# A Mamba-2 scan stage: decays spread over the partitions by broadcast loads, and one convolution by taps on ScalarE and VectorE

## The chip, the cores and the metric

The kernel runs on one core of one Trainium2 chip. The metric is the device time of one execution, in microseconds (us); the median of three executions is compared. The core has TensorE (PE; its weight loads are shown as PEld), VectorE (DVE), ScalarE (ACT), GpSimd (POOL) and SyncE (SP, which only issues DMAs here), each with its own in-order instruction queue. They wait for each other through counters.

## What is computed

The input has 32 sequences of 256 tokens of 64 channels. Three layers follow:

- a convolution with 9 taps to 128 features, scaled by a window norm, tanh, bias, relu (248 tokens are left per sequence);
- a Mamba-2 block with a residual, with 4 heads of 64, a state of 64, and a causal convolution of 4 taps ahead of a SiLU;
- a mixture of 16 experts (top 2) with a shared expert and a last feed-forward layer.

The change is in the Mamba-2 block, whose heart is, cut to what matters:

```python
zxbcdt = x @ in_proj_w                       # z 256, xBC 384, dt 4
xBC = silu(causal_conv_4_taps(xBC) + conv_b) # per channel
dt = softplus(dt + dt_bias); decay = exp(-dt * exp(A_log))
def step(h, inp):                            # over the tokens, per head
    h = decay_t * h + (dt_t * x_t) outer B_t
    y_t = h @ C_t
y = (ys + D_skip * x) * silu(z); y = rms_norm(y) * norm_w
out = y @ out_proj_w
```

## The kernel before

The tokens are cut into 16 units of 2 sequences. A sequence has 248 tokens, that is 2 chunks of CH = 124. A unit goes through four stages, each one step behind the other: `a` (the 9-tap convolution, tanh, norm), `b` (the projections, the 4-tap convolution, dt), `c` (the scan and the output projection) and `d` (second norm, router logits, shared expert, scatter of rows to the experts). Step t works on unit t in stage a, t-1 in b, t-2 in c, t-3 in d. The loops `for t in range(STEPS)`, one per engine (PE line 911, ACT 1149, POOL 1368, DVE 1748), write out by hand the order of each engine's work in a step. After the steps come the expert phase (139 blocks of 128 rows) and the last layer.

The scan has no recurrence in the chip's sense. For each sequence (a "part" n of the unit, n = 0, 1) the kernel forms the scores G = B C^T (`scores`, line 760), multiplies them by the product of decays between the two tokens, and takes the product with the inputs (`mix`, 790). The decay products are made as follows. `decays` (774) does 8 TensorE transposes per part: each spreads one head's decays of one chunk (a column of `dec`) over all partitions, in PSUM. `long_scans` (1500) runs two scans of 2x248 elements over them (`state = state * decay + diagonal`), which gives L0 (tokens of chunk 0 against all 248), and `short_scans` (1509) four of 124 elements for L1 (chunk 1 against itself). A `keep` mask of POOL (line 1323) stops the state at the start of each sequence. `decayed_scores` (1516) multiplies L0 (992 elements) and L1 (496 elements) by G, to M0 and M1.

The order of VectorE's step is: long scans of part 0, `dt_first` (1453), `x_rest` (1430), short scans and decayed scores of part 0, `bc_taps` (1480), `dt_rest` (1465), `skip_add` of part 0 (1526), scans and decayed scores of part 1, `stats` of unit a (1442), logits and slots or the first half of `choose` (these two in alternate steps), `skip_add` of part 1, `x_scale`, `shared_out`, `sum_squares`, the second half of `choose` (every other step), `hn_rest` (1435), `mean_squares`, `residual` (which waits for a power on POOL, line 1338), `new_stats`. From `stats` POOL makes the reciprocal deviation (`rstd_of`, 1308), ACT the norm (`norm`, 1051), PE transposes it (`hn_transposes`, 697), ACT copies it (`hnT_copy`, 1069) and DVE takes the low part (`hn_rest`); the next step's projections need it. From `skip_add` of part 1 POOL does `gate` (1326, line 1332), then PE `output` (808, line 814) and after it, in PE's order, `hn_transposes`. POOL's order has `rstd_of` ahead of `gate` of part 1.

The 4-tap convolution: for B and C it is done by taps (`bc_begin` on ACT, `bc_taps` on DVE, `bc_silu` on ACT). For x, two parts of 128 channels each, the taps are folded into the projection weights (`w_tap`), and `projection` (725) does 4 taps x 3 products (high and low parts) = 12 matmuls of 496 columns for each x part (k = 0, 1), and 3 for each z part (k = 2, 3). Lines 650 to 652 are the three matmuls of `product`.

## Time and profile before

| what | value |
|---|---|
| median of 3 executions | 1030.62 us (1022.71, 1030.62, 1031.51) |
| profiled execution, its own time | 1024.98 us |
| its span in the profile | 1023.1 us |
| PE, DVE, POOL, ACT busy | 905.9, 724.6, 587.5, 502.3 us |

Roughly, the steps run to 585 us, the experts to 885 us, and the last layer to the end. "Busy" is the time in which an engine's instructions ran. In the timeline a line's second number is the time in which a run of equal instructions was under way; the next instruction of an engine can begin up to some 0.08 us ahead of the end shown for the last. "Issue" is time for which the profile shows no wait.

### The profile page before, as it was taken

How to read it: one execution, taken by the hardware profiler on the slowest of the kernel's cores; microseconds unless marked ns; L12 is line 12 of the kernel's file. 1: busy time of each engine (PE TensorE's matmuls, PEld its weight loads, DVE VectorE, ACT ScalarE, POOL GpSimd, SP SyncE). 2: the span in 40 equal slices, each digit the busy share in tenths (PEclk: the TensorE clock that was granted, in tenths of full speed). 3: DMA queues.
4: the chain of work that ended last, by engine and by line, in shares of the span. 5: the costliest groups of instructions: out<-in, count | busy, mean ns of one | idle time of the engine just before them, and what ended most of it. 6: DMA issues, size and time to landing. Idle time of an engine off the chain costs nothing.

```text
span 1023.1 us, 22359 instructions
## 1 busy us (share of the span) xinstructions
PE 905.9 (89%) x6324; PEld 790.4 (77%) x6325; DVE 724.6 (71%) x2092; ACT 502.3 (49%) x1259; POOL 587.5 (57%) x649
## 2 busy tenths in 40 slices
PE   4697999999999999999874369999999998669998
PEld 3576877877877787887654269999999998558887
DVE  5357799888889989888874335555555554599993
ACT  3333555554555555555322125555555554555653
POOL 5435455777778777777646454444444444365551
PEclk9989999999999999999966679999999999879999
DMA  7400000110100110000095112232221221224332
GB/s 180 90 11 11 1 11 12 31 31 22 30 17 27 32 31 27 16 19 16 18 275 158 40 44 68 78 85 67 65 67 55 58 64 54 56 81 114 97 101 51
DMA packets 72057, 59.12 MB, mean 58 GB/s; under 512 B 19169, under 2 KB 61468, under 8 KB 71985
## 3 DMA queue, kind: packets, MB, share of 16 engines
q1 hardware_dynamic: 63440, 41.88, 15.9%
q0 software_dynamic: 8544, 16.34, 4.8%
q8 instruction: 37, 0.61, 0.3%
q14 instruction: 36, 0.29, 0.1%
HBM read 35.62 MB, written 23.81 MB: 58 GB/s over the span
## 4 chain that ended last, share of the span: by engine, by line
PE 48%; DVE 24%; issue 15%; POOL 8%; another core or an unknown queue 1%; ACT 1%; DMA 1%; SPq 0%; DVEq 0%; POOLq 0%; ACTq 0%
PE psum L967 13%; PE psum L952 13%; DVE arena L1504 4%; DVE arena L1852 4%; PE psum L650 3%; POOL x_slots L1362 3%; PE psum L651 3%; PE psum L652 3%; PE psum L785 2%; PE psum L802 2%; DVE h_all L1552 2%; DVE arena L1857 2%; PE psum L961 2%; POOL arena L1338 2%; DVE arena L1512 2%
## 5 line engine op out<-in xcount | busy, mean ns | idle before, releaser
L1189 ACT ACTIVATE arena<-psum,arena 128x128 f32<-128x128 f32 x556 | 159.0, 369 | 155.9 <-PE psum L952 131.9
L1395 POOL DMA_INDIRECT y_tokens<-arena x139 | 136.8, 984 | 161.0 <-DVE arena L1802 117.1
L952 PE MATMUL psum<-arena 128*128 128x128 f32 x1112 | 154.5, 283 | 27.2 <-DVE arena L1795 15.7
L952 PEld LDWEIGHTS psum<-arena 128*128 128x128 f32 x1112 | 139.9, 198 | 29.1 <-DVE arena L1789 15.3
L967 PE MATMUL psum<-arena 128*128 x1112 | 156.4, 284 | 0.4 <-issue 0.4
L1362 POOL DMA_INDIRECT x_slots<-arena,idx x128 | 128.0, 1000 | 34.6 <-issue 34.3
L967 PEld LDWEIGHTS psum<-arena 128*128 128x128 f32 x1112 | 137.6, 194 | 7.4 <-issue 0.6
L1789 DVE COPY arena<-arena 128x644 f32 x139 | 75.4, 542 | 72.1 <-issue 65.6
L1795 DVE TENSOR_SCALAR arena<-psum,lng,lnb 128x128 f32<-128x128 f32 x139 | 56.9, 409 | 52.5 <-PE psum L961 40.8
L1504 DVE TENSOR_TENSOR_SCAN arena<-psum,arena 124x496 f32<-124x496 f32 x64 | 72.5, 1175 | 11.9 <-PE psum L785 7.8
L1332 POOL TENSOR_TENSOR arena<-arena 128x496 f32<-128x496 f32 x32 | 40.0, 1251 | 34.6 <-DVE arena L1532 34.6
L1009 PE MATMUL psum<-w_f,arena 128*124 128x128 f32 x512 | 58.4, 273 | 0.0
L1009 PEld LDWEIGHTS psum<-w_f,arena 128*124 128x124 f32 x512 | 57.1, 187 | 0.1
L650 PE MATMUL psum<-hnT_hi,w_tap_hi 128*128 128x496 f32 x128 | 53.7, 420 | 0.0
L1306 POOL TENSOR_TENSOR arena<-euler,arena 124x16 f32<-124x16 f32 x16 | 46.4, 2902 | 12.4 <-DVE arena L1462 12.0
L651 PE MATMUL psum<-hnT_lo,w_tap_hi 128*128 128x496 f32 x128 | 50.8, 396 | 0.0
L652 PE MATMUL psum<-hnT_hi,w_tap_lo 128*128 128x496 f32 x128 | 50.4, 394 | 0.0
L1207 ACT ACTIVATE arena<-arena,nm,rs 124x128 f32<-124x128 f32 x64 | 26.5, 485 | 47.9 <-POOL nm L1407 47.9
L1802 DVE TENSOR_TENSOR arena<-psum,arena 128x128 f32<-128x128 f32 x139 | 39.1, 281 | 13.9 <-PE psum L967 10.5
L1064 ACT ACTIVATE arena<-h_all,nm,rs 124x128 f32<-124x128 f32 x64 | 26.4, 485 | 43.6 <-POOL r1p L1349 43.6
L1321 POOL TENSOR_TENSOR arena<-euler,arena 124x16 f32<-124x16 f32 x16 | 46.9, 2928 | 1.3
L1405 POOL TENSOR_TENSOR rs<-ve,minus_half 124x4 f32<-124x4 f32 x16 | 16.3, 1022 | 52.1 <-DVE ve L1871 52.1
(283 smaller groups left out, 2215.8 us busy)
## 6 DMA issues: line engine op xcount, KB each, us to landing
arena<-x_slots SPq DMA_DIRECT2D x139, 64.5 KB
arena<-y_tokens SPq DMA_DIRECT2D x16, 448.0 KB
arena<-in_x SPq DMA_DIRECT2D x16, 256.0 KB, 3.2
out_tokens<-arena SPq DMA_DIRECT2D x16, 224.0 KB
y_tokens<-arena POOLq DMA_INDIRECT x139
x_slots<-zero_src SPq DMA_DIRECT2D x33, 64.5 KB, 4.2
moe_all<-in_x SPq DMA_DIRECT2D x4, 512.0 KB, 5.8
x_slots<-arena,idx POOLq DMA_INDIRECT x128
```

The costliest lines, as they stand in the source:

```text
L650: nc.tensor.matmul(o, stationary[0], moving[0], start=start, stop=False)
L651: nc.tensor.matmul(o, stationary[0], moving[1], start=False, stop=False)
L652: return nc.tensor.matmul(o, stationary[1], moving[0], start=False, stop=stop)
L952: last = nc.tensor.matmul(psum[:, 2 + b.q % 2, k * 128:(k + 1) * 128], w1_blk[b.q % 4][:, k * 128:(k + 1) * 128], hT[b.q % 2], start=True, ...
L967: last = nc.tensor.matmul(psum[:, 4 + c.q % 2, 0:F], EHT[c.q % 2][:, k * 128:(k + 1) * 128], w2[:, ds(at + k * F, F)], start=(k == 0), sto ...
L1009: last = nc.tensor.matmul(psum[0:CH, 5 + u % 2, j * F:(j + 1) * F], FH[u % 2][:, k, j * CH:(j + 1) * CH], w_f2[:, k, :], start=(k == 0), s ...
L1189: last = nc.scalar.activation(EHT[t.q % 2][:, k * 128:(k + 1) * 128], psum[:, 2 + t.q % 2, k * 128:(k + 1) * 128], ACT.Silu, bias=w1_blk[t ...
L1362: nc.gpsimd.indirect_dma_start(out=x_slots, out_offset=bass.IndirectOffsetOnAxis(ap=idx[g % 3][:, col:col + 1], axis=0), in_=x_st[u % NXS] ...
L1395: nc.gpsimd.indirect_dma_start(out=y_tokens, out_offset=bass.IndirectOffsetOnAxis(ap=xb[t.q][:, F:F + 1].bitcast(i32), axis=0), in_=YO[t.q ...
L1504: V.tensor_tensor_scan(L0.rearrange("p h t -> p (h t)")[:, g * 2 * L:(g + 1) * 2 * L], psum[0:CH, 5 + g, 0:2 * L], diag2.rearrange("p h t ...
L1789: nc.vector.tensor_copy(w1_blk[t.q % 4], w1[:, ds(at, EW)]).then_inc(X.w1_ready, 1)
L1795: nc.vector.tensor_scalar(hT[t.q % 2], psum[:, 6 + t.q % 2, 0:BLK], lng[:, 0:1], lnb[:, 0:1], ALU.mult, ALU.add).then_inc(X.hT_ready, 1)
```

## The change

1. **Decays by DMA.** PE's 16 transposes of a step go. Instead `dec_rows` does one transpose of all 16 columns of `dec` (4 chunks x 4 heads) to 16 rows; ACT copies them twice into `dec_st`; DVE's `cum_decays` turns one copy into cumulative products; SP stores both to DRAM (`decays_out`, four small DMAs) and loads them back, spread over 124 partitions, as DB[n] (`decays_in`, two DMAs of 124 x 1488 floats a step).
2. **Off-diagonal block as a product.** Per part one scan of 8x124 elements over DB gives the two diagonal blocks for the 4 heads. The block of chunk 0 against chunk 1 is the scan's last column times the cumulative products of chunk 1, in four `scalar_tensor_tensor` of 124 elements.
3. **The second x part by taps.** `projection(b, 1)` becomes 3 matmuls, and moves up to just behind `conv`; `x1_begin` and `x1_silu` on ACT and `x1_taps` on DVE do the convolution. Only 128 channels are folded now, and `conv_w` is loaded to 128 channels only (256 instead of 768 KB).
4. **Order.** DVE: `stats(a)` moves behind logits, slots, choose and `cum_decays`; `skip_add(c, 0)` behind the scan of part 1. ACT: `x1_silu` ahead of `tanh(a)`, `squares` and `dec_copy` between `tanh` and `relu`. POOL: `decay_of` ahead of `add_bias` and `gate`; the mask is gone.
5. **Buffers.** Tg and Sq are gone: `skip_add` writes Yg, `gate` works in place, the squares go to XT. SP's last loads of expert weights wait for `pr_ready` instead of `yg_ready`.

```diff
@@ SP
-                for u in range(2, UNITS):
-                    load(u)
+                def decays_out(b):
+                    sp.wait_ge(S.cum_ready, b + 1)
+                    for n in range(2):
+                        later(sp, db_here[n], 16 * (b - 1))
+                    for n in range(2):
+                        sp.dma_start(dec_rows_of[b % 2, n, 0:8, :], dec_st[b % 2][8 * n:8 * n + 8, 0, :])\
+                            .then_inc(S.dec_stored, 16)
+                        sp.dma_start(dec_rows_of[b % 2, n, 8:12, :], dec_st[b % 2][8 * n + 4:8 * n + 8, 1, :])\
+                            .then_inc(S.dec_stored, 16)
+                def decays_in(b):
+                    sp.wait_ge(S.dec_stored, 64 * (b + 1))
+                    for n in range(2):
+                        later(sp, S.m_ready, 2 * (b - 1) + n + 1)
+                        sp.dma_start(DB[n].rearrange("p r t -> p (r t)"),
+                                     rows(dec_rows_of[b % 2, n].rearrange("r t -> (r t)"), CH)
+                                     .rearrange("p o t -> p (o t)"))\
+                            .then_inc(db_here[n], 16)
+                for t in range(UNITS + 1):
+                    if t + 2 < UNITS: load(t + 2)
+                    if t >= 1: decays_out(t - 1); decays_in(t - 1)
...
-                sp.wait_ge(S.yg_ready, 2 * UNITS)
+                sp.wait_ge(S.pr_ready, UNITS)
@@ PE
+                def dec_rows(b, a):
+                    pe.wait_ge(S.dec_ready, b + 1)
+                    if a is not None:
+                        pe.wait_ge(S.tanh_done, a + 1)
+                    nc.tensor.transpose(psum[0:16, 1, 0:CH], dec[b % 2].rearrange("p j h -> p (j h)"),
+                                        ident[0:CH, 0:CH]).then_inc(S.dect_psum, 1)
...
-                    if c is not None: decays(c, 0); scores(c, 0)
+                    if c is not None: scores(c, 0)
...
                     if a is not None: conv(a, b)
+                    if b is not None: projection(b, 1, None)
...
-                    if c is not None: scores(c, 1); decays(c, 1)
+                    if c is not None: scores(c, 1)
...
-                    if b is not None: projection(b, 1, None); projection(b, 2, None); x_rows(b)
+                    if b is not None: dec_rows(b, a)
+                    if b is not None: projection(b, 2, None); x_rows(b)
@@ ACT
+                    if b is not None: x1_begin(b)
                     if b is not None: bc_silu(b)
                     if d is not None: hhT_copy(d)
-                    if a is not None: tanh(a); relu(a)
+                    if b is not None: x1_silu(b)
+                    if a is not None: tanh(a)
                     for n in parts_at(t): squares(n)
-                    if b is not None: silu(b, 1)
+                    if b is not None: dec_copy(b)
+                    if a is not None: relu(a)
@@ DVE
+                def x1_taps(b):
+                    dve.wait_ge(S.x1_begun, b + 1)
...
+                    for back in range(1, KC):
+                        o = x1[:, :, back:]
+                        last = V.scalar_tensor_tensor(o, u[:, :, 0:L - back], cw_x1[:, KC - 1 - back:KC - back], o,
+                                                      ALU.mult, ALU.add)
...
+                def scans(c, n):
+                    dve.wait_ge(db_here[n], 16 * (c + 1))
+                    o = DB[n][:, 0:8, :].rearrange("p r t -> p (r t)")
+                    V.tensor_tensor_scan(o, o, diag8.rearrange("p r t -> p (r t)"), 0.0, ALU.mult, ALU.add)\
+                        .then_inc(S.scan_done, 1)
...
+                    V.tensor_tensor(M[:, 0:3:2, :, :], DB[n][:, 0:8, :].rearrange("p (k h) t -> p k h t", h=NH),
+                                    G[:, 0:3:2, :].unsqueeze(2).broadcast_to([CH, 2, NH, CH]), ALU.mult)
+                    for h in range(NH):
+                        last = V.scalar_tensor_tensor(M[:, 1, h, :], G[:, 1, :], DB[n][:, h, CH - 1:CH],
+                                                      DB[n][:, 8 + h, :], ALU.mult, ALU.mult)
...
+                def cum_decays(b):
+                    dve.wait_ge(S.dect_copied, b + 1)
+                    v = dec_st[b % 2][:, 1, :]
+                    V.tensor_tensor_scan(v, v, ones_col[64:80, :].to_broadcast([16, CH]), 1.0, ALU.mult, ALU.mult)\
+                        .then_inc(S.cum_ready, 1)
...
-                    if c is not None: long_scans(c, 0)
+                    if c is not None: scans(c, 0)
                     if b is not None: dt_first(b)
                     if a: x_rest(a)
-                    if c is not None: short_scans(c, 0); decayed_scores(c, 0)
+                    if c is not None: decayed_scores(c, 0)
...
-                    if c is not None: skip_add(c, 0); long_scans(c, 1); short_scans(c, 1); decayed_scores(c, 1)
-                    if a is not None: stats(a)
+                    if b is not None: x1_taps(b)
+                    if c is not None: scans(c, 1); skip_add(c, 0); decayed_scores(c, 1)
...
+                    if b is not None: cum_decays(b)
+                    if a is not None: stats(a)
                     if c is not None: skip_add(c, 1)
```

## Rows read from the trace of the kernel before

**Rows 1.** the page: busy time by engine, and the chain that ended last

```profile
PE 905.9 (89%) x6324; PEld 790.4 (77%) x6325; DVE 724.6 (71%) x2092; ACT 502.3 (49%) x1259; POOL 587.5 (57%) x649
PE 48%; DVE 24%; issue 15%; POOL 8%; another core or an unknown queue 1%; ACT 1%; DMA 1%; SPq 0%; DVEq 0%; POOLq 0%; ACTq 0%
```

**Rows 2.** one stretch: us; PE, PEld, DVE, ACT, POOL busy; PEclk; DMA

```profile
100.00:400.00 300.00, 292.57 (x1950) 238.92 (x1949) 259.23 (x732) 161.50 (x340) 208.16 (x229) 1.00 0.07 22
```

**Rows 3.** chain that ended last, first scans of steps 3 and 15

```profile
98.22 1.10 DVE arena L1504
...
460.34 2.17 DVE arena L1504 x2
```

**Rows 4.** timeline of step 7: start us, us, engine, line, operation, count [idle before]

```profile
218.51 2.26 DVE L1504 TENSOR_TENSOR_SCAN arena<-psum,arena 124x496 f32<-124x496 f32 x2
...
228.56 1.06 PE L785 MATMUL psum<-ident,arena 124*124 124x124 f32 x8
...
230.07 2.27 DVE L1504 TENSOR_TENSOR_SCAN arena<-psum,arena 124x496 f32<-124x496 f32 x2 [0.66 <-PE psum L785]
...
230.80 0.48 PE L650 MATMUL psum<-hnT_hi,w_tap_hi 128*128 128x496 f32 x1
...
232.26 1.31 DVE L1512 TENSOR_TENSOR_SCAN arena<-psum,ident 124x124 f32<-124x124 f32 x4
...
233.60 1.19 DVE L1521 TENSOR_TENSOR arena<-arena,psum 124x992 f32<-124x992 f32 x1
...
234.71 0.66 DVE L1523 TENSOR_TENSOR arena<-arena,psum 124x496 f32<-124x496 f32 x1
...
235.29 0.87 DVE L1446 BATCH_NORM_STATS2 arena<-h_all 124x6 f32<-124x128 f32 x4
...
236.66 0.19 POOL L1311 TENSOR_SCALAR neg<-arena 124x4 f32<-124x4 f32 x1 [0.63 <-DVE arena L1450]
...
238.18 0.20 POOL L1314 TENSOR_TENSOR nmn<-neg,arena 124x4 f32<-124x4 f32 x1
...
238.95 0.86 DVE L1532 SCALAR_TENSOR_TENSOR arena<-arena,d_col,psum 128x248 f32<-128x248 f32 x2
...
239.88 1.25 POOL L1332 TENSOR_TENSOR arena<-arena 128x496 f32<-128x496 f32 x1 [1.50 <-DVE arena L1532]
...
241.36 1.91 PE L814 MATMUL psum<-arena 128*124 128x128 f32 x16
...
244.35 0.68 DVE L1437 TENSOR_TENSOR hnT_lo<-psum,hnT_hi 128x496 fp32r<-128x496 f32 x1 [1.52 <-ACT hnT_hi L1072]
...
248.90 2.27 DVE L1504 TENSOR_TENSOR_SCAN arena<-psum,arena 124x496 f32<-124x496 f32 x2
```

**Rows 5.** groups by line, 100:400 us: busy, mean ns | idle before

```profile
L1485 DVE SCALAR_TENSOR_TENSOR arena<-psum,cw_bc,arena 128x494 f32<-128x494 f32 (+2 forms) x30 | 21.9, 729 | 0.7
...
L1552 DVE SCALAR_TENSOR_TENSOR h_all<-psum,arena,h_all 124x128 f32<-124x128 f32 x40 | 11.3, 345 | 11.5 <-POOL arena L1338 11.5
```

**Rows 6.** DMA issues by line (KB each, median us to landing)

```profile
h_all<-in_conv_w SPq DMA_DIRECT2D x1, 768.0 KB, 5.8
```

**Rows 7.** line 513 (x loads), issue to landing; SyncE's timeline, a small load

```profile
DMA to landing us min/median/max: 2.6/3.2/5.4
...
6.33 0.35 SPq L536 DMA_DIRECT2D cb<-in_conv_b  x1
```

**Rows 8.** the view of Rows 2 while expert weights load

```profile
520.00:530.00 10.00, 6.55 (x30) 4.92 (x31) 8.15 (x29) 3.15 (x7) 7.75 (x11) 0.50 1.04 318
```

**Rows 9.** timeline of step 0, VectorE and TensorE

```profile
24.61 1.19 DVE L1635 TENSOR_REDUCE h_all<-moe_all 128x16 f32<-128x1024 f32 x1
...
25.86 1.82 PE L672 MATMUL psum<-h_all 128*124 128x8 f32 x8 [8.03 <-DVE h_all L1635]
```

**Rows 10.** timeline of step 2, TensorE after a long gap

```profile
88.54 3.32 PE L814 MATMUL psum<-arena 128*124 128x128 f32 x16 [3.41 <-POOL arena L1332]
```

**Rows 11.** timeline of step 17, second part's long scans

```profile
533.48 2.27 DVE L1504 TENSOR_TENSOR_SCAN arena<-psum,arena 124x496 f32<-124x496 f32 x2 [4.09 <-remote]
```

180 lines of the change are left out of this document (85 added, 95 removed).

## The prediction

> **What bounds the kernel now.** I read the page first: TensorE is busy for 89% and the chain that ended last lies on it for 48%, on VectorE for 24% [rows 1]. The change touches only the steps, so the next view is the busy time of 100 to 400 us: TensorE 292.6 of 300 us, VectorE 259.2, POOL 208.2, ScalarE 161.5, and a granted clock of 1.00, which is 2.4 GHz [rows 2]. By that TensorE is the bound and its relief worth the more. But the chain of waits enters each step on VectorE's long scans, at 98.22 in step 3 and 460.34 in step 15: (460.34 - 98.22) / 12 = 30.18 us a step [rows 3]. So I walked through one step in the timeline, from its first scan at 218.51 to the next one at 248.90 [rows 4], with 218.51 as zero. VectorE works almost without a gap to `skip_add` of part 1 at 20.44. Then a chain goes round: `gate` on POOL (21.37 to 22.62), `output` on TensorE at 22.85, the transposes of hn, their copy, `hn_rest` at 25.84; 4.55 us more to the next step, with 1.16 us in which VectorE waits for POOL's power (11.5 us in 10 steps [rows 5]). VectorE and TensorE arrive at `skip_add` together. Both are a bound, and a relief of TensorE alone is lost unless VectorE's part of the ring gets shorter too.
>
> **What the change takes from TensorE.** 16 transposes (8 in 1.06 us, twice: 2.1) and 9 of 12 matmuls of an x part. The folded products follow each other at 0.23 us, so 2.1 us [rows 4]. One transpose comes, 0.3 at most. TensorE's 292.6 / 300 x 30.18 = 29.4 us a step fall to 25.5. It is then no bound.
>
> **What it does to VectorE's order.** Before, a part costs from its long scans at 230.07 to `stats` at 235.29, that is 5.22 us: 2.19 long, 1.34 short scans, 1.11 for 992 products, 0.58 for 496 [rows 4]. Two parts: 10.44. After, each part has
>
> - one scan of 992 elements. Two of 496 take 2.19 from start to start, four of 124 take 1.34, so 2.2 ns an element with little for an instruction: 2.13 us. It reads SBUF where these read PSUM; I take no difference, between -0.3 and +0.3;
> - 992 products as before, 1.11;
> - four `scalar_tensor_tensor` of 124. The nearest row is line 1552, four of 128 in about 1.1 us (mean 0.345, overlapping) [rows 5]: 1.04.
>
> That is 4.28, twice 8.56. The taps are the twin of `bc_taps`, 3 x 0.729 [rows 5]: 2.17. `cum_decays` is a scan of 124, 0.33 as one of the short ones. Sum 11.06: VectorE gains 0.62 us of work a step. The wait of 0.66 for the transposes goes [rows 4]. So `skip_add` of part 1 comes at 20.44 + 0.62 - 0.66 = 20.4, where it was. Bounds for this term: -0.8 to +1.0.
>
> **What the move of stats does.** This is the step that costs most. `stats` used to end at 236.57, 2.4 us ahead of `skip_add`, and POOL had used the time for `rstd_of` (236.66 to 238.38) [rows 4]. Now `stats` ends as `skip_add` begins. `rstd_of` stands ahead of `gate` of part 1 in POOL's queue: neg, add, power and product, 1.8 us from the end of `stats`, so `gate` starts at 20.4 + 1.8 = 22.2 and not at 21.37. `gate` takes 1.25, to 23.5. From the end of `gate` (241.13) to `hn_rest` (244.35) it is 3.2 us [rows 4], which makes 26.7 against 25.84. The rest of the step, 4.55, is unchanged. **+0.9 us a step**, bounds 0 (if stats come early enough) and +1.5. It counts in steps 2 to 15, which have all of stages a, b and c: 14 x 0.9 = **+12.6**.
>
> ScalarE gets 1.2 us more (one activation from SBUF, two copies of 16 rows) and is busy for only 54% [rows 2]. It delays `tanh(a)` by some 2 us behind `x1_silu`; bias, relu and the square of part 0 follow, then `silu(b, 2)`, which frees the bank for `shared_up`. I get 17.2 for `shared_up`, against 17.0, and the end of `mix` of part 1 at 20.6: just not late. POOL loses a 0.22 us product. The cost of both is 0, up to +1 if the cover is gone.
>
> **The round trip by DMA.** Its cover is the time from `cum_decays` to the next step's scan. `cum_decays` ends at 20.4 - 1.25 = 19.15, the next step begins at 31.3: 12.1 us. SP then issues four small stores at 0.35 each, and the last must land; the x loads land 2.6 us after issue at best with 256 KB [rows 7], so 1.05 + 2.3 = 3.4. Then SP issues the loads, 738 KB each. The nearest row is the broadcast load of `conv_w` to 128 partitions, 768 KB, 5.8 us beside other loads [rows 6]. 9.2 us in all: hidden, with 2.9 us to spare. Ends: 7.9 us (2.3 us and 738 KB at the 318 GB/s of rows 8 for the load) and some 15 us, below. Part 1's load lands some 3 us later and has 11 us more. The x loads behind it on SP's queue have a whole step of slack.
>
> **The first steps.** In step 0 the row squares start at 24.61 and the window sums on TensorE run from 25.86 to 27.7 [rows 9]. `stats(0)` took the 1.2 us ahead of them, from 23.4, and now stands behind: row squares from 23.4 (1.2), windows (1.9), one small operation (0.2), 26.7: **+3.3**, on the path, as TensorE has nothing else. In step 1 the cover of the round trip is short: no stage c, so from `cum_decays` to the next step it is 1.25 + 1.8 + 1.65 (norm) + 2 = 6.7 us against 9.1: **+2.4**, bounds 0 and +8. The smaller `conv_w` load and fold save nothing: what step 0 waits for is POOL's power for the scale.
>
> **The drain.** Step 17 has no stage b, and TensorE runs at half clock (0.50, 1.2 GHz [rows 8]). There four long and eight short scans become two scans of 992: -2.7 us, the products +1.0, and the transposes ahead of the second part go. VectorE sat 4.09 us before its scans there, for a releaser that the trace gives as remote [rows 11]; it may stay or go. I take **-2.5**, bounds 0 and -6.6. The last weight loads wait some 3 us longer; I cost that at nothing, as the steps end at 553 us by VectorE's order and the experts begin some 30 us later, and 3 us if that cover is gone.
>
> **Sum.** 12.6 + 3.3 + 2.4 - 2.5 = +15.8 us. The profiled execution took 1024.98, so it would take 1041; the median of the three is 5.6 us above it. I put the sum on the median: **1047 us**. Its own range is 1036 to 1058.
>
> **Rivals.**
>
> *The round trip is late.* If the broadcast loads don't spread over all 16 DMA engines, their rate is a share of the 318 GB/s: on 4 engines 80 GB/s, 9.3 us for 738 KB. With 3.4 for the stores and 2.3 for the fixed part this is 15.0 against a cover of 12.1, so 2.9 us late in each step, with every engine behind it, as `x_rest` and `dt_first` stand behind the scan. If one engine does as well as under `conv_w`, it is about 0.5. Taking 1.5: 14 x 1.5 = +21, and 2 more in step 1: 1070. For it: 124 partitions where `conv_w` had 128, and part 1's load in the same queues. Against it: the `conv_w` row.
> The Trainium skill (DMA: Bandwidth & Descriptors, "Why a DMA increments its semaphore by 16 and not by 1") states that a DMA is split over the largest number of engines up to 16 that divides the slowest dimension of both sides; for 124 that is 4. By that rule this rival is what happens; no row here shows a large load over 124 partitions.
>
> *TensorE was the bound after all (the other side).* If `rstd_of` doesn't delay `gate`, and VectorE's waits for others than POOL's power go, a step is VectorE's own time: 259.2 / 300 x 30.18 = 26.1, + 0.6 + 1.15 + 0.8 for the chained small operations = 28.6. It decides once `nmn` is ready before `skip_add` ends, that is if `stats` ends 0.9 us or more ahead of it. 14 x -1.5 = -21, with the ends +3.2 and -2.5: 1010. For it: 97.5% busy [rows 2]. Against: VectorE had only some 3.2 us of idle time a step.
>
> *Nothing gained, nothing lost.* The bounds of VectorE's terms go my way by 0.8 a step: 1047 - 11 - 4 = 1032.
>
> *The clock.* After 3.41 us without work `output` took 3.32 us at half clock, against 1.91 [rows 4, 10]. With 5.5 us of idle time a step such a gap could come ahead of `output` each time: +1.9 with the transposes, 14 x 1.9 = 27, 1074. The gaps that I find (ahead of the transposed decays, ahead of `shared_up`, ahead of `output`) are 2 us at most, which speaks against it.
> The Trainium skill (TensorE: Matmul & The Clock Gate, "HAM oscillation") warns of idle gaps longer than those I find; by its rule the clock stays, as I forecast.
>
> **How the numbers follow.** Forecast 0.40, late round trip 0.28, no effect 0.13, TensorE as bound 0.12, clock 0.07. The range is 1026 to 1080: it takes in the late round trip short of its worst and the case of no effect, and leaves out that of 1010. About 1% is what a measurement of this kernel tells from no change. Faster than 1020: 0.12. Between 1020 and 1041: 0.21 (no effect, and the lower end of the forecast). Slower: 0.67.
>
> **What would show it.** Right: steps of 31 us between first scans, TensorE busy for 80 to 85% of 100 to 400 us, VectorE for 86 to 89%, `gate` of part 1 starting right behind `rstd_of`, `stats(0)` at 26 to 27 us. The first scan of a step waits for a DMA: the late round trip. Steps under 29.5 us: the second rival. I am wrong if `gate` follows `skip_add` directly, or if the granted clock leaves 1.00 in this stretch.

## The result, and the profile after

The changed kernel takes 1080.13 us (median of 4 runs, 1078.59 to 1084.64) against 1029.45 us (1022.71 to 1031.51) in the same rounds: a ratio of 1.051, 95% interval 1.045 to 1.057. Forecast were 1047 us and a range of 1026 to 1080, whose upper end the measured median passes by 0.1. The direction was right; of the size, 16 us were forecast and 51 came. In the table of experiments below, one execution of the kernel e11 that took 2840.51 us, in the chip's slower state, is left out of its median.

The page of the profile of the changed kernel, busy time by engine and the chain that ended last, and under it the view of [rows 2] for the same 100 to 400 us:

```profile
PE 882.5 (82%) x5940; PEld 767.0 (71%) x5941; DVE 746.0 (69%) x2092; ACT 518.0 (48%) x1307; POOL 618.0 (57%) x633
...
PE 44%; DVE 25%; issue 11%; DMA 9%; POOL 8%; another core or an unknown queue 1%; ACT 1%; SPq 1%; DVEq 0%; POOLq 0%; ACTq 0%
```

```profile
100.00:400.00 300.00, 256.83 (x1589) 207.78 (x1589) 246.66 (x674) 156.60 (x335) 198.35 (x197) 0.92 0.19 66
```

TensorE gave up 36 us in this stretch and VectorE has 13 us less too, so no engine is at its limit: the kernel runs along a chain of waits. The granted clock left 1.00, and DMA, which had 1% of the chain, has 9%. As in [rows 3], the first scans of steps 3 and 15 give the step, here by VectorE's timeline:

```profile
107.31 2.22 DVE L1547 TENSOR_TENSOR_SCAN arena<-arena 124x992 f32<-124x992 f32 x1
...
504.96 2.22 DVE L1547 TENSOR_TENSOR_SCAN arena<-arena 124x992 f32<-124x992 f32 x1
```

(504.96 - 107.31) / 12 = 33.14 us a step, against 30.18 before: 35.5 us of the 54 by which the profiled spans differ (1077.0 and 1023.1). Step 3 begins 9.1 us later than before, steps 15 and 16 lose another 12, and the rest gives 3 back. Steps 3 to 5, in which GpSimd has no scatters yet, take 30.8 to 32.5 us, steps 6 and 8 to 11 take 32 to 33, and steps 7 and 12 to 16 take 33.8 to 36.3.

Two groups by line, the scans on VectorE and the transpose of the decays on TensorE (busy, mean ns | idle before it, releasers):

```profile
L1547 DVE TENSOR_TENSOR_SCAN arena<-arena 124x992 f32<-124x992 f32 x32 | 71.1, 2221 | 18.8 <-DMA arena<-dec_rows_of 12.7 <-issue 6.1
```

```profile
L800 PE MATMUL psum<-ident,arena 124*16 124x124 f32 x16 | 5.4, 340 | 42.5 <-POOL arena L1356 36.2 <-ACT arena L1061 6.2
```

Scans wait 12.7 us for the broadcast loads. TensorE stands 42.5 us ahead of 16 small transposes, `dec_rows`, of which 36.2 for GpSimd's power in `decay_of`. The chain of waits shows how long the first load of a pair takes, from the end of the stores to its landing, ahead of the next step's scan (start, us, what):

```profile
290.81 10.92 DMA arena<-dec_rows_of
```

10.9 us where I took 5.8 from [rows 6]. The second load is issued 0.3 us behind the first and its last part lands some 17 to 20 us after its issue (I had forecast 3 us behind the first); that is in time, since the second scan of steps 2 to 16 never waits. And GpSimd's timeline in step 13, under it VectorE's in the same microseconds:

```profile
434.53 2.02 POOL L1375 TENSOR_SCALAR neg<-MV 124x4 f32<-124x4 f32 x1 [0.34 <-issue]
...
444.46 0.97 POOL L1393 DMA_INDIRECT x_slots<-arena,idx  x1 [0.30 <-issue]
445.73 2.96 POOL L1393 DMA_INDIRECT x_slots<-arena,idx  x1 [0.30 <-issue]
...
449.02 2.93 POOL L1356 TENSOR_TENSOR arena<-euler,arena 124x16 f32<-124x16 f32 x1
```

```profile
434.35 2.22 DVE L1547 TENSOR_TENSOR_SCAN arena<-arena 124x992 f32<-124x992 f32 x1
...
445.69 2.22 DVE L1547 TENSOR_TENSOR_SCAN arena<-arena 124x992 f32<-124x992 f32 x1
```

Read the two together: `neg` on 124x4 numbers takes 2.02 us and ends at 436.55, the scan over it at 436.57. A scatter that takes 0.97 us takes 2.96 when it begins under the second scan. Between 200 and 560 us 14 of GpSimd's instructions are 1.1 to 2.0 us longer than others of their line, and all 14 begin under one of these scans. Before, none is between 200 and 500 us: the same `neg` there took 0.19 us though it began 0.18 us into a long scan, which read PSUM:

```profile
218.69 0.19 POOL L1344 TENSOR_SCALAR neg<-MV 124x4 f32<-124x4 f32 x1 [0.35 <-issue]
```

The next reading is TensorE's timeline behind the wait in step 13. The products follow each other at 0.42 to 0.56 us, not at the 0.23 of [rows 4]: half clock, which also comes in step 8 after a wait of only 2.12 us (the granted clock is 0.50 from 283.5 to 286.5 us).

```profile
452.01 0.38 PE L800 MATMUL psum<-ident,arena 124*16 124x124 f32 x1 [5.20 <-POOL arena L1356]
452.04 0.76 PE L670 MATMUL psum<-hnT_hi,w_in_hi 128*128 128x496 f32 x1
452.60 0.61 PE L671 MATMUL psum<-hnT_lo,w_in_hi 128*128 128x496 f32 x1
```

```profile
283.58 0.38 PE L800 MATMUL psum<-ident,arena 124*16 124x124 f32 x1 [2.12 <-POOL arena L1356]
```

The last reading follows the delay to the end of the step. Behind GpSimd's bias and first gate stands ScalarE's `silu(b, 2)`, behind it TensorE's `shared_up` (line 873) and `mix` of part 1 (line 818), and behind that VectorE's `skip_add` of part 1 (line 1576), from which the second gate and the next step follow. Step 13 again, TensorE and VectorE:

```profile
455.63 2.83 PE L873 MATMUL psum<-arena,w_s 128*128 128x496 f32 x4 [0.29 <-ACT arena L1111]
```

```profile
459.96 0.86 DVE L1576 SCALAR_TENSOR_TENSOR arena<-arena,d_col,psum 128x248 f32<-128x248 f32 x2 [2.92 <-PE psum L818]
```

Starts in step 13 of GpSimd's bias (`add_bias`) and of the other two, in us from the step's first scan, here and in kernels of the next section:

| kernel | bias | `shared_up` | `skip_add` of part 1 |
|---|---|---|---|
| before | 11.6 | 17.0 | 20.4 |
| the change | 17.6 | 21.3 | 25.6 |
| e1 split loads | 17.6 | 21.3 | 24.9 |
| e5b operand in PSUM | 13.8 | 17.4 | 20.9 |
| e9 scatters behind | 13.2 | 17.0 | 20.4 |

Forecast were 17.2 for `shared_up` and 20.4 for `skip_add`.

### The profile page after: what moved, and what is told of

The parts are those of the page before. It is cut to its first block, busy times and chain, and to the rows that moved or that the text cites. A ratio compares the mean times of both kernels' runs of the same rounds, so it can differ in the third digit from the quotient of the medians.

```text
span 1077.0 us, 21748 instructions
## 1 busy us (share of the span) xinstructions
PE 882.5 (82%) x5940; PEld 767.0 (71%) x5941; DVE 746.0 (69%) x2092; ACT 518.0 (48%) x1307; POOL 618.0 (57%) x633
## 4 chain that ended last, share of the span: by engine, by line
PE 44%; DVE 25%; issue 11%; DMA 9%; POOL 8%; another core or an unknown queue 1%; ACT 1%; SPq 1%; DVEq 0%; POOLq 0%; ACTq 0%
PE psum L985 12%; PE psum L970 12%; DMA arena<-dec_rows_of 7%; DVE arena L1898 4%; PE psum L670 4%; PE psum L671 3%; PE psum L672 3%; DVE arena L1547 3%; POOL x_slots L1393 3%; DVE arena L1903 2%; PE psum L979 2%; DVE arena L1556 2%; DVE arena L1559 1%; PE psum L816 1%
## 5 line engine op out<-in xcount | busy, mean ns | idle before, releaser
L1393 POOL DMA_INDIRECT x_slots<-arena,idx x128 | 135.9, 1062 | 34.3 <-issue 34.3
L1547 DVE TENSOR_TENSOR_SCAN arena<-arena 124x992 f32<-124x992 f32 x32 | 71.1, 2221 | 18.8 <-DMA arena<-dec_rows_of 12.7
L816 PE MATMUL psum<-arena 124*64 124x248 f32 x256 | 45.3, 427 | 6.8 <-DVE arena L1559 6.8
L1848 DVE TENSOR_TENSOR arena<-psum,arena 128x128 f32<-128x128 f32 x139 | 39.1, 281 | 12.5 <-PE psum L985 6.6
L873 PE MATMUL psum<-arena,w_s 128*128 128x496 f32 x64 | 38.0, 725 | 11.9 <-ACT arena L1111 11.9
L1898 DVE SCALAR_TENSOR_TENSOR arena<-arena,VAL,moe_all 124x128 f32<-124x128 f32 x64 | 43.9, 747 | 2.6 <-DMA arena<-y_tokens 2.6
```

What stands on the lines that cost most here:

```text
L816: nc.tensor.matmul(o, Xd[:, 2 * n, h * HD:(h + 1) * HD], M[:, 0:2, h, :], start=True, stop=False)
L1393: nc.gpsimd.indirect_dma_start(out=x_slots, out_offset=bass.IndirectOffsetOnAxis(ap=idx[g % 3][:, col:col + 1], axis=0), in_=x_st[u % NXS] ...
L1547: V.tensor_tensor_scan(o, o, diag8.rearrange("p r t -> p (r t)"), 0.0, ALU.mult, ALU.add)\
L1898: ins = V.scalar_tensor_tensor(g[:, j, :], GY[u % 2][:, 2 * j, :], VAL[:, 0, 4 * u + j:4 * u + j + 1], MOE[:, 512 * u + j * F:512 * u + (j ...
```

## The experiments

A "step" is the mean between the first scans of steps 3 and 15, "stall" the idle time of TensorE ahead of the 16 `dec_rows`. Both are of the one profiled execution, which lies within 5 us of the median except in e1 (10.0 above it), e14 (7.3 below) and e17 (7.4 above). Each kernel was timed in the same rounds as the kernel before. In the third group the kernel before itself took 991.64 us instead of 1026 to 1029, so times are compared by ratio.

| kernel | us | ratio (95%) | step | stall |
|---|---|---|---|---|
| before | 1029.45 | 1 | 30.18 | - |
| the change | 1080.13 | 1.051 (1.045, 1.057) | 33.14 | 42.5 |
| e1 split loads | 1076.31 | 1.050 (1.045, 1.054) | 34.06 | 55.3 |
| e2 decays only | 1113.13 | 1.086 (1.081, 1.091) | 36.33 | 56.0 |
| e3 taps only | 1060.93 | 1.035 (1.030, 1.040) | 33.03 | - |
| e4 stats first | 1089.73 | 1.064 (1.058, 1.069) | 34.24 | 21.1 |
| e5b operand in PSUM | 1046.96 | 1.020 (1.014, 1.027) | 31.68 | 18.8 |
| e6b power early | 1080.44 | 1.052 (1.046, 1.057) | 34.07 | 12.5 |
| e7b rows late | 1088.43 | 1.056 (1.049, 1.063) | 34.06 | 0.0 |
| e8b stats first | 1071.59 | 1.041 (1.036, 1.047) | 34.03 | 12.7 |
| e9 scatters behind | 1018.44 | 1.025 (1.020, 1.030) | 31.63 | 13.0 |
| e10 scan ahead | 1055.02 | 1.060 (1.053, 1.067) | 34.42 | 8.3 |
| e11 stats too | 1067.63 | 1.073 (1.066, 1.080) | 35.98 | 9.2 |
| e12 all | 1033.63 | 1.042 (1.035, 1.048) | 32.99 | 25.7 |
| e13 stats and scatters | 1028.16 | 1.002 (0.998, 1.006) | 30.98 | 14.7 |
| e14 rows early | 1049.67 | 1.023 (1.015, 1.030) | 31.80 | 30.3 |
| e15 scan behind | 1037.03 | 1.011 (1.004, 1.019) | 31.28 | 32.8 |
| e16 whole loads | 1090.03 | 1.061 (1.053, 1.069) | 34.72 | 12.0 |
| e17 half scans | 1027.45 | 1.000 (0.997, 1.002) | 31.01 | 14.6 |
| e18 operand in PSUM | 1026.80 | 1.001 (0.998, 1.004) | 30.64 | 17.4 |

**First group: each part by itself.** The split is the one that the kernel uses for its token rows:

```diff
-                        sp.dma_start(DB[n].rearrange("p r t -> p (r t)"),
-                                     rows(dec_rows_of[b % 2, n].rearrange("r t -> (r t)"), CH)
+                        for p0, p1 in ((0, 112), (112, CH)):
+                            sp.dma_start(DB[n].rearrange("p r t -> p (r t)")[p0:p1, :],
+                                         rows(dec_rows_of[b % 2, n].rearrange("r t -> (r t)"), p1 - p0)
```

> The changed kernel with each broadcast load of decay rows split into partitions 0 to 111 and 112 to 123. Theory A (the loads run on few DMA engines, 10.4 to 11.5 us each, and end behind their cover): a load takes 5 to 6.5 us, the 12.7 us of VectorE idle before the first scans (arena from dec_rows_of) fall below 1 us, and the time falls by those 13 to 18 us from 1080, to 1062 to 1067. Theory B (the step is set by TensorE waiting for GpSimd's power behind the scatters, and the late load only fills time that is lost anyway): the load is as fast, but the time stays within 4 us of 1080. If the stretched instructions (a GpSimd scatter 2.95 us instead of 0.97) come from the long loads, they vanish and the steps of 33.8 to 36.3 us become 32: 1055 or less.

1.050: theory B; against the change the time is 4 us less, which is within the noise of both. The loads are cured. In the profile the change's loads run at 102 GB/s with 0.30 of the 16 DMA engines busy, the split ones at 257 GB/s with 0.90 (window: us; PE, PEld, DVE, ACT, POOL busy; clock; DMA share; GB/s; the change first; GpSimd's scatters run beside both):

```profile
291.00:301.50 10.50, 9.52 (x74) 8.88 (x74) 7.87 (x29) 5.97 (x13) 7.36 (x10) 1.00 0.30 102
```

```profile
291.00:296.50 5.50, 5.50 (x52) 5.20 (x48) 3.87 (x8) 2.84 (x7) 3.22 (x4) 1.00 0.90 257
```

The scans' 18.8 us of idle time become 0.2, and the stall grows from 42.5 to 55.3 instead. Steps 3 to 5 take 31.1 us each, those from the sixth on 34.1 to 35.9. Two things follow: something else makes the step, and it comes with GpSimd's scatters. And the last sentence of the expectation is wrong: the stretched instructions don't come from the long loads, since `neg` is now 2.02 us in nearly every step. The two stretches of a step, 1.8 us of `neg` and 1.9 to 2.0 of a scatter or of the power, now stand in all steps from the seventh on: bias at 17.5 to 17.6, `shared_up` at 21.2 to 21.3, where the change has them so late in four steps of those.

Next the two parts of the change apart. The decays alone, with both x parts folded again and in the old places:

```diff
-        w_tap2 = take_pair("w_tap", [F, KC, 128])
+        w_tap2 = take_pair("w_tap", [F, KC, 256])
...
-                    if b is not None: projection(b, 1, None)
...
-                    if b is not None: projection(b, 2, None); x_rows(b)
+                    if b is not None: projection(b, 1, None); projection(b, 2, None); x_rows(b)
...
-                    if b is not None: x1_taps(b)
```

> The changed kernel with both x parts folded into weights again: the decay parts of the change alone. Theory A (the loss is the decays' round trip and the order around it): 1070 to 1090, since TensorE gets 3.9 us a step back and VectorE loses 2.3 us a step of taps. Theory C (the taps carry the loss, since they stand ahead of the second scan and of the rows of x): 1045 to 1055.

And the taps alone, on the kernel before:

```diff
                     if b is not None: dt_rest(b)
+                    if b is not None: x1_taps(b)
                     if c is not None: skip_add(c, 0); long_scans(c, 1); short_scans(c, 1); decayed_scores(c, 1)
```

> The kernel before with the taps for the second x part alone, placed as in the change. VectorE gets 2.25 us a step, TensorE is relieved of 3.9. Theory A (VectorE's order sets the end of each step, and nothing of the folded projection's time stood on the path): plus 1 to 2.3 us a step over 15 steps, 1045 to 1065. Theory D (TensorE, busy 97.5% before, was the bound): minus 1 to 3 us a step, 985 to 1015.

Both parts lose, and not as either theory has it. The decays alone give 1.086, 23 us above theory A's upper end: the stall is 56 us, and the 9 matmuls that the taps would have saved stand right behind it. The folded products average 0.52 to 0.58 us between 243 and 430 us, against 0.39 to 0.41 at full clock. The taps alone cost 34 us, in theory A's range for the time; its 2.9 us a step are above the 2.3 of the same theory: all of VectorE's 2.25 and some more. TensorE's relief bought nothing: it has 25 us less to do between 100 and 400 us, and the clock falls to 0.92. The rest is seen behind VectorE's longer row: TensorE waits up to 3.3 us for the short scans of part 1, whose banks the rows of x need, and `shared_up` behind it takes 3.1 us on the average of steps 3 to 15 and not 1.93 as in each step before. So VectorE's `skip_add` waits for `mix`, 14.3 us in 9 steps from 100 to 400 us, against 2.9 in 10 before. Together the parts cost 51 us and not 34 + 86. That the taps take TensorE's work away where the decays make it wait would explain this; no run shows it by itself.

e4 is the change with whole loads, the statistics back in their place and relu ahead of the copy of the decays:

```diff
                     if c is not None: scans(c, 1); skip_add(c, 0); decayed_scores(c, 1)
+                    if a is not None: stats(a)
...
-                    if a is not None: stats(a)
...
-                    if b is not None: dec_copy(b)
                     if a is not None: relu(a)
+                    if b is not None: dec_copy(b)
```

> The changed kernel with the statistics back ahead of the router's logits on VectorE, and for it relu ahead of the copy of the decays on ScalarE. By the recorded term (0.9 us a step over 14 steps, statistics to rstd to second gate): 1066 to 1070. By the rival that the second gate no longer ends the step (the late loads and TensorE's stall at the rows of the decays do): 1078 to 1085, the copy of the decays some 0.5 to 1 us later and the load with it.

The recorded term did not show: 10 us slower, 5 beyond the rival's range. Relu had to move too and waits for GpSimd's bias, so the decays leave later: the scans wait 48.6 us for their loads and not 12.7, and the chain has 15% on these loads, 7% in the change. With whole loads what ends a step here is the round trip and not the second gate.

**Second group: the port and GpSimd's queue.** From here on all kernels have split loads, e16 excepted. e5b reads the scans' second operand from PSUM. That operand is then rows of x and not the diagonal, so e5b (and e18 below) computes something else than the reference; TensorE's rows of x also wait for the scans there.

```diff
-                    V.tensor_tensor_scan(o, o, diag8.rearrange("p r t -> p (r t)"), 0.0, ALU.mult, ALU.add)
+                    other = psum[0:CH, 5:7, :].rearrange("p k t -> p (k t)")[:, 0:8 * CH]
+                    V.tensor_tensor_scan(o, o, other, 0.0, ALU.mult, ALU.add)
```

> The kernel with split loads, and the diagonal operand of both scans read from banks 5 and 6 of PSUM, which hold the rows of x, in place of the tile in SBUF. So the decay matrices hold other numbers, and the router may spread its rows otherwise; the 15 steps up to the last scan are what is compared. Theory P (a scan of VectorE with both inputs in SBUF keeps GpSimd out for its whole 2.22 us: in the changed kernel all of the stretched GpSimd instructions between 230 and 560 us begin under such a scan and end with it or soon after): no GpSimd instruction is stretched any more, the wait at the rows of the decays falls from 5.7 to some 3.5 us, and the steps from the sixth on from 35.1 to 32.5 to 33.5 us. Theory Q (the stretched instructions come from something else, the traffic or the descriptors): they stay, with steps of 35. The scans themselves take 2.2 to 2.4 us either way.

1.050 becomes 1.020, the step 31.7, most steps 31.1. The scan itself takes as long as ever, and `neg` is short again (the split kernel's line first, then this one's: duration ns min/median/max):

```profile
L1376 POOL TENSOR_SCALAR neg<-MV x16: 191/2020/2026, 104.9 to 615.0; 124x4 f32<-124x4 f32 x16
```

```profile
L1377 POOL TENSOR_SCALAR neg<-MV x16: 189/190/292, 106.5 to 578.3; 124x4 f32<-124x4 f32 x16
```

```profile
L1550 DVE TENSOR_TENSOR_SCAN arena<-arena,psum 124x992 f32<-124x992 f32 x32 | 70.8, 2212 | 0.0
```

The same traffic and work, one operand in another memory: 29 us. That is theory P. No GpSimd instruction between 100 and 560 us is longer than its like by 0.3 us or more, though 53 begin under a scan. `shared_up` starts 3.8 us earlier in step 13 than with split loads alone, which is the sum of the two stretches. Steps 3 to 5, without scatters, take 31.1 us with the stretch and without. So the price is in where GpSimd's work stands, not in VectorE's time.

The Trainium skill (SBUF — State Buffer, "Who interferes with whom") states it: a VectorE instruction with two inputs in SBUF and a GpSimd instruction that reads SBUF lock each other out, and who issues first keeps the port for the whole instruction. The trace agrees in both directions, but for a GpSimd power that holds up no scan and that no scan holds up once it has begun (last section): in the change two VectorE operations (line 1669) that take 0.49 us together take 2.67 at 252.14, from the start to the end of GpSimd's bias and gate.

e6b moves the power ahead of two scatters:

```diff
-                    if v is not None and v < UNITS - 5: scatter(v, (2, 3))
+                    if v is not None and v < UNITS - 5: scatter(v, (2,))
                     if b is not None: decay_of(b)
+                    if v is not None and v < UNITS - 5: scatter(v, (3,))
```

> The kernel with split loads, and GpSimd's power of the decays moved ahead of two of the four scatters. Theory S (from the sixth step on the rows of the decays hold TensorE up behind GpSimd's four scatters): the power starts 2.6 us earlier or more, the wait of TensorE falls from 5.7 to 3 us or less, and the steps from 35.1 to 32.5: 1045 to 1055. Theory T (the second gate or the late statistics set the step): 1070 to 1077.

e7b adds to this:

```diff
-                    if b is not None: dec_rows(b, a)
                     if b is not None: projection(b, 2, None); x_rows(b)
+                    if b is not None: dec_rows(b, a)
```

> As the power early, and the rows of the decays behind the third projection and the rows of x on TensorE, so that 2 us of work stand in the place of the wait. Theory S: another 1 to 2 us a step, 1020 to 1040, as long as the split loads, now begun some 2 us later, still land before the next scan. If the load is late again, the first scans wait for it and the time is that of the power early or above.

e8b adds the edit of e4 to e6b:

> As the power early, with the statistics ahead of the router's logits and relu ahead of the copy of the decays. By the recorded term (0.9 us a step from the statistics to the second gate), now that neither the load nor the stall at the rows of the decays is in its way: 10 to 13 us below the power early. If GpSimd's second gate is not what ends a step: within 4 us of it.

Theory S falls: the power starts earlier, TensorE waits 0.4 to 1.3 us at `dec_rows` in steps 6 to 15, and the step is 34.1 as before the edit. The wait reappears one product later (TensorE's and ScalarE's timeline of the kernel with the power early, rows that waited):

```profile
319.24 0.27 PE L801 MATMUL psum<-ident,arena 124*16 124x124 f32 x1 [0.80 <-ACT arena L1062]
325.35 3.54 PE L874 MATMUL psum<-arena,w_s 128*128 128x496 f32 x4 [4.28 <-ACT arena L1112]
```

```profile
323.02 0.63 ACT L1068 ACTIVATE h_all<-arena 124x512 f32<-124x512 f32 x1 [3.06 <-POOL arena L1335]
```

`shared_up` waits for ScalarE's `silu(b, 2)`, which stands behind relu and the first square, which wait for GpSimd's bias and first gate, still behind four scatters and a stretched `neg`. The power was one of three things held up; this names theory G, which the third group tests. Part of the gain also went into the clock: `shared_up` starts at 19.4 us of a step and not at 21.3, but behind its longer wait it takes 2.7 to 3.7 us in steps 6 to 15, where it takes 1.93 at full clock. The rows late change nothing for the better (one more miss): the step is 34.1 again, and the time 8 us more, with overlapping intervals. The statistics first give 9 us, 7.3 of them in the one step in which VectorE's window sums stood ahead of them, and nothing in the steps that GpSimd sets.

**Third group: GpSimd's row of work.**

```diff
                     if c is not None: gate(c, 0)
+                    if v is not None and v < UNITS - 5: scatter(v, (3,))
```

> Split loads, and on GpSimd the second pair of scatters behind the first gate, so that power, bias and first gate all come 2.6 us earlier. Theory G (from the sixth step on a step is GpSimd's row of work: powers for the new row norms, stretched by 2.0 us under the first scan, exponential, scatters, power, bias, first gate, and behind that ScalarE, the shared projection on TensorE and the second mix): the steps fall from 35 to 32 to 33, 1035 to 1050. That the power alone, moved, gave nothing speaks for it, since bias and gate stayed behind four scatters there. If something outside GpSimd sets the 35 us, 1070 to 1080 again.

1.025 against 1.050: theory G holds. (By the difference to the kernel before of the same rounds it is 27 us against 49.) The steps with scatters fall from 35 to 31.3, though `neg` is still stretched to 2.02 us, and `shared_up` and `skip_add` start where they did before the change, at 17.0 and 20.4 us. So either the port or the order takes away the same 22 to 30 us: GpSimd's row was too long for the step by about the two stretches, and one of the two remedies suffices. The kernel before has the same four scatters ahead of its bias, so it is their place together with the stretches, or with the power that the change put there, that is at fault; the power alone was not put back behind the gate.

e10 is e9 with the first scan of a step at the end of the step before:

```diff
-                    if c is not None: scans(c, 0)
+                    if c == 0: scans(c, 0)
...
+                    if b: scans(b, 0)
                     if a is not None: hn_rest(a)
```

> As the scatters behind, and the first scan of a step moved to the end of the step before, into the 1.5 us that VectorE waits there for the copy of the normed rows, and where GpSimd waits too. Theory P (the port) expects the 2.02 us instruction at a step's start back at 0.2, VectorE's path 1.4 us shorter at most: 1 to 2 us a step below the scatters behind, 1015 to 1035, unless the split load lands behind the scan's new place, about 1 us sooner than now; then no gain or a loss of up to 1 us a step.

e11 adds the edit of e4, and e12 on top of that:

```diff
                     if c is not None: scores(c, 1)
+                    if b is not None and t > 2: dec_rows(b, a)
...
                     if c is not None: scans(c, 1); skip_add(c, 0); decayed_scores(c, 1)
+                    if b is not None and t > 2: cum_decays(b)
```

> As the scan ahead, with the statistics ahead of the router's logits and relu ahead of the copy of the decays. With the port and GpSimd's queue out of the way the recorded term (0.9 us a step over 14 steps) should show, and the 7 us of the step in which VectorE's window sums stand ahead of the statistics: 15 to 20 us below the scan ahead, 1000 to 1015. If the steps are set elsewhere by then: 7 us.

> As the statistics too, with the rows of the decays and their cumulative product ahead of the router's work from the third step on, so that the round trip starts about 2 us earlier. If the first scans wait for the loads in the kernel with the statistics too, it takes that wait away, up to 1 us a step; if they don't, it changes nothing (within 4 us), or costs where TensorE stands at the rows of the decays with the router behind it.

The scan ahead is a miss, and dear, though `neg` is back at 0.19 us as expected. The scan waits 2.25 us for its load in the step looked at (9.5 us in all), and `mean_squares` stands behind it, which frees the bank for the next step's scores: TensorE waits there 23.0 us in 9 steps between 100 and 400 us, against 7.5 us in 10 in the kernel with the scatters behind. The dt sums behind are late too. With the statistics first it grows worse, since the decays leave later; sending them earlier gets 3.0 us a step back of the 4.4 that both edits cost.

**Fourth group: what is left.**

e13 is e9 with the edit of e4.

> Split loads, the second pair of scatters behind the first gate, statistics ahead of the router's logits and relu ahead of the copy of the decays; the scan in its place. The kernel with scatters behind alone took 1.025 of before, steps of 31.27, and 38.1 from the second to the third. By the recorded term (0.9 us a step, statistics to gate): steps of 30.3 to 30.5 and 30.7 to 31 there, together 20 us less, a ratio of 1.00 to 1.01. If something else holds the steps at 31.2: only the one step, 7 us less, 1.017 to 1.02. If the round trip, begun later behind relu, is late: steps of 32 and more, first scans waiting for the loads, 1.03 or more.

1.002: level with before. The steps of 31.3 become 30.3 to 30.8 from the fifth on, but for one of 32.4. From the start of `skip_add` of part 1 to the next step's first scan it is 10.8 us in most steps of e9, and 10.0 in e13 and before: the recorded 0.9 us. It was right.

e14 adds the edit of e12 to e13. e15 is e13 with:

```diff
-                    if c is not None: scans(c, 0)
                     if b is not None: dt_first(b)
                     if a: x_rest(a)
-                    if c is not None: decayed_scores(c, 0)
+                    if c is not None: scans(c, 0); decayed_scores(c, 0)
```

> As the kernel before it in this list, with the rows of the decays ahead of the router's work on TensorE and the cumulative product ahead of the statistics from the third step on. If first scans wait for the loads there, they no longer do here and the time is 5 to 15 us less; if they don't, it is within 4 us, or up to 6 us more, since the 0.41 us product stands ahead of the statistics again.

> As the kernel with statistics and scatters, with a step's first scan behind the first sums for dt and the low part of x, 1.0 us later. By the port GpSimd's power for the row norms then starts ahead of the scan and is not stretched, its row of work is up to 2 us earlier, and the sums for dt are 2.2 us earlier: 0 to 1.5 us a step less. If neither is on the path: within 4 us.

Both are misses. First scans waited 3.7 us for loads in the whole of e13, so there was nothing for the rows early to gain, and they cost 22 us, far above the 6 allowed. The scan behind costs 9 us. The stall at `dec_rows` is 30.3 and 32.8 us in them and 14.7 in e13, nearly all of it a wait for ScalarE's work ahead of the transpose; in e14 `skip_add` of part 1 then starts at 20.8 to 24.3 us of a step and not at 20.4. What took the 9 us of e15 stays open.

e16 is e13 with the loads whole, as in the change.

> As the kernel with statistics and scatters, with the two broadcast loads whole again, as in the change. By the recorded picture's missing term (a load takes 11 us instead of 5.8, against a cover that ends 1 to 2 us sooner in a step of 30.4): first scans wait 2 to 4 us in every step, 30 to 50 us more than with split loads. If the cover is long enough: within 8 us, most of it in the first steps (5.4 us at the second scan before).

Here the loads show their whole price: 61.9 us, above the 30 to 50 expected. The scans wait 61.8 us in all, 56.8 of it the first scan of a step:

```profile
L1548 DVE TENSOR_TENSOR_SCAN arena<-arena 124x992 f32<-124x992 f32 x32 | 71.1, 2222 | 61.9 <-DMA arena<-dec_rows_of 61.8
```

In the changed kernel splitting them brought 4 us, which is in the noise, here 62. What a fault costs depends on which others stand in front of it.

```diff
-                    V.tensor_tensor_scan(o, o, diag8.rearrange("p r t -> p (r t)"), 0.0, ALU.mult, ALU.add)
+                    V.tensor_tensor_scan(o[:, 0:4 * CH], o[:, 0:4 * CH], diag[:, 0:4 * CH], 0.0, ALU.mult, ALU.add)
...
                     if b is not None: dt_first(b)
+                    if c is not None: second_half(c, 0)
```

This is e17, e13 with each scan in two halves. e18 is e13 with the edit of e5b.

> As the kernel with statistics and scatters (1.002 of before), with each scan in two halves of 496 columns, the sums for dt between the halves of the first. By the port GpSimd's first instruction of a step is stretched to 1.0 us instead of 2.02, its power for the row norms starts ahead of the second half, and the wait of ScalarE for it (3.85 us) falls by 1 to 2 us. If that wait is on the path: 0.5 to 1 us a step less, 0.985 to 0.995 of before. If not: the halves' own start costs of some 0.1 us each, 1.00 to 1.01.

> As the kernel with statistics and scatters, with the diagonal operand of both scans read from PSUM again, so that the decay matrices hold other numbers; the steps are what is compared. By the port: no stretched instruction; steps of 29.5 to 30.4 instead of 30.4 to 30.6 where GpSimd's first instruction was on the path, and of 30.4 to 30.6 where it was not, since VectorE alone is busy for some 26 us of them.

In e17 `neg` falls to 0.99 us as expected, and the time doesn't move; in e18, with no stretch at all, it doesn't either (1.001; the step is 30.6 and not 31.0). Once GpSimd's row is short enough, the port costs nothing that these times show. No version beat the kernel before. e13 and e17, which compute what the reference does, are level with it within 0.6%.

## Why the prediction was wrong

- *What bounds the kernel.* Right: not TensorE alone. The taps alone (1.035) show that relieving TensorE at VectorE's expense costs all of VectorE's share. The rival that TensorE alone was the bound is refuted.
- *VectorE's work, 11.06 us a step.* Right in its terms: scan 2.22 (2.13 forecast), taps 2.25 (2.17), `cum_decays` 0.41 (0.33), four products 1.10 (1.04).
- *The scan reads SBUF where the old ones read PSUM: "I take no difference, between -0.3 and +0.3".* **This is the first step that failed.** For VectorE it is right to 0.1 us. But I priced the operand on its own engine only; it locks GpSimd out for up to 2 us, twice in most steps of the kernel with split loads and in steps 7 and 13 to 16 of the change. With it fails the sentence on ScalarE's and GpSimd's row: "I get 17.2 for `shared_up` ... and the end of `mix` of part 1 at 20.6: just not late". `shared_up` starts at 21.3 in steps 7 and 13 to 15 and `skip_add`, which waits for `mix`, at 24.7 to 25.6. With the operand in PSUM it is 17.4, near the forecast, and taking the lock away brought 29 us.
- *GpSimd: "the cost of both is 0, up to +1 if the cover is gone".* **The second.** I counted the product that it loses and not what `decay_of`, put ahead of bias and gate, makes them wait for: they start behind four scatters, as before, and now behind a product and a power too. Unstretched, bias starts at 13.8 us of a step and not at 11.6, which costs `shared_up` only 0.4 to 1.0 us; but it leaves no room for the stretches, which then reach the end of the step. With the second pair of scatters behind the gate the ratio fell from 1.050 to 1.025. These two are one fault, GpSimd's row of work, and their gains don't add: with both remedies (1.001) the time is that of one (1.002).
- *Statistics to rstd to second gate, +0.9 a step.* Right, where `skip_add` is on time: in step 8 of the change the gate starts at 291.69, right behind `rstd_of`, as said. Where `skip_add` comes late, `rstd_of` is done by then. With GpSimd's row mended the step went from 31.3 to 30.4 when the statistics went back; by first scans that pair is 15 us apart from step 2 to 17, 6.0 of them in the step with the window sums.
- *The round trip, 9.2 us against a cover of 12.1.* **The third.** The load takes 10.4 to 11.5 us in the steps, not 5.8; the row of `conv_w`, with 128 partitions, was the wrong neighbour. It made scans wait 12.7 us in the change, and 61.8 in e16, where the other faults are mended. My rival had the mechanism with 9.3 + 2.3 us, and I gave it 0.28 against the row of another shape. By the rule of the Trainium skill that I cited with it (DMA: Bandwidth & Descriptors, "Why a DMA increments its semaphore by 16 and not by 1"), 124 partitions run on 4 engines: the trace agrees, with 102 GB/s at a DMA share of 0.30, which is 4.8 of 16 engines with the scatters beside, and 257 GB/s at 0.90 when 112 and 12 partitions go apart.
- *The first steps, +3.3 and +2.4.* The first is right to 0.1 (the first norm at 29.86, before at 26.55). The second is the round trip again: 5.41 us.
- *The clock: gaps of 2 us at most, so it stays.* **Wrong** in both halves. The gaps at `dec_rows` are up to 5.2 us (5.7 with split loads), and one of 2.12 already left TensorE at half clock for some 3 us. The sentence on the Trainium skill there (TensorE: Matmul & The Clock Gate, "HAM oscillation") drew the wrong comfort: the page warns of gaps longer than this one, and here the measurement decides. What the clock cost in all was not isolated; `shared_up`, which is on the path, takes 2.3 us on the average of steps 3 to 15 of the change and 1.93 before.
- *The drain, -2.5.* The span behind step 17's first scan is 500.9 us against 504.0: -3.1 us.
- *The sums.* Two small terms are not worked out in the text: the 3.2 in the sum for TensorE as bound, where the term above it is 3.3, and the 4 in 1047 - 11 - 4. Neither changes the result.
- *The signs.* The granted clock left 1.00, which was named as a sign of being wrong, and first scans waited for DMAs, the sign of the late round trip. TensorE is busy for 85.6% of 100 to 400 us (80 to 85 forecast), VectorE for 82% (86 to 89).

How the 51 us divide among these faults can't be said, since their gains don't add. What is shown is that split loads, the scatters behind and the statistics first together take all of it away (e13).

## What to carry to other kernels

In this kernel an operand moved from PSUM to SBUF had its price on the engine that shares the port, not on the one that reads it: ask what GpSimd has under each long VectorE instruction, and whether it can wait. When an instruction is moved in a queue, walk every instruction behind it to the one that ends the step, with the loops that only run in later steps. And where several faults stand on one ring, removing one shows almost nothing (4 us for the split loads here, 62 once the others were gone): mend the likeliest together, then take each away again. To find such a delay, measure the start of a few instructions of the chain from the first one of the step, in several steps and kernels: a shift of 3.8 us stands out there that busy times hide.

## What was not expected of the hardware

- GpSimd's indirect DMA, and not only its arithmetic, is held up by a VectorE scan with two inputs in SBUF: 2.96 us instead of 0.97, in 4 of the 14 cases.
- A GpSimd power that has begun before the scan is not stretched. In the kernel with the power early it runs from 316.13 to 319.06, across the start of a scan at 317.33, and the scan takes its 2.22 us as ever. In the change one that begins 0.1 us into a scan, at 517.76, takes 4.84 us and not 2.93.
- TensorE at half clock after a wait of 2.12 us; it was busy for 8.9 of the 10 us from 270 to 280.
